# Gated attention plus mixture of experts: one expert's rows sorted by products instead of two, and both its layers run first

## What is computed

```python
x = x + tanh(g_xattn) * smoothquant_expert(layernorm(x), gate_up, down)   # int8-like, per batch element
s = layernorm(x)                                   # 1024 rows of 256
gates = softmax(s @ w_gate)                        # 8 experts
e = argmax(gates); slot = number of earlier tokens with the same e; kept while slot < 128
h = gelu(dispatched[e] @ w1[e])                    # 128 x 256 @ 256 x 1024
y = h @ w2[e]                                      # 128 x 1024 @ 1024 x 256
x = x + tanh(g_ffn) * gates[e] * y                 # for the kept tokens
```

## Time and profile before

| | us |
|---|---|
| three runs, median (lowest, highest) | 118.71 (117.54, 119.16) |
| the profiled execution | 118.51 |
| its span | 116.7 |
| PE busy in the span | 101.5 (87%) |
| DVE busy | 86.3 (74%) |
| ACT busy | 76.2 (65%) |
| POOL busy | 53.9 (46%) |
| PE's share of the chain that ended last | 38% |

### The profile page before, as it was taken

One profiled execution on the slowest core, in us unless ns is written; L12 is line 12 of the kernel. 1 busy time (PEld: TensorE's weight loads), 2 busy tenths in 40 slices (PEclk: granted clock), 3 DMA queues, 4 the chain that ended last, 5 costly groups with the idle time before them and its releaser, 6 DMA issues.

```text
span 116.7 us, 2279 instructions
## 1 busy us (share of the span) xinstructions
PE 101.5 (87%) x770; PEld 88.0 (75%) x770; DVE 86.3 (74%) x229; ACT 76.2 (65%) x158; POOL 53.9 (46%) x117
## 2 busy tenths in 40 slices
PE   0979679999889889987999969999999999999930
PEld 0459358988557657886999759899999989999820
DVE  5637989899987899981049759969688696939540
ACT  0464789999896989894737739585573739376000
POOL 7858765669968878867730000621030303011041
PEclk9999999999999999999999999999999999999999
DMA  3999998999984903379226999899999900101011
GB/s 73 345 308 323 150 198 314 338 367 373 364 293 89 341 25 139 134 205 336 101 83 205 287 351 323 308 350 280 346 297 361 325 0 0 51 0 45 0 45 45
DMA packets 16074, 24.86 MB, mean 213 GB/s; under 512 B 1352, under 2 KB 13641, under 8 KB 15040
## 3 DMA queue, kind: packets, MB, share of 16 engines
q1 hardware_dynamic: 14208, 21.60, 59.5%
q0 software_dynamic: 768, 2.08, 4.9%
q10 hardware_dynamic: 1088, 1.05, 2.8%
HBM read 20.50 MB, written 4.28 MB: 212 GB/s over the span
## 4 chain that ended last, share of the span: by engine, by line
PE 38%; POOL 14%; DMA 13%; DVE 12%; ACT 11%; issue 7%; SPq 2%; POOLq 1%; DVEq 0%
PE bk L1133 19%; PE bk L1145 10%; POOL slot_rows L406 6%; DMA x<-in_x 6%; DMA gr<-slot_rows 5%; PE bk L1147 5%; DVE am L706 3%; ACT wide_a L519 3%; POOL row L392 2%; DMA slot_rows<-row,slot 2%; ACT wide_b L528 2%; POOL sc L350 2%; PE bk L1159 2%; PE bk L998 1%; DVE am L762 1%
## 5 line engine op out<-in xcount | busy, mean ns | idle before, releaser
L471 POOL DMA_INDIRECT out<-scrow,gr x8 | 8.6, 1075 | 45.9 <-DVE scrow L926 44.5
L1133 PE MATMUL bk<-rows_w,w_sb 128*128 128x128 f32 x192 | 22.8, 275 | 0.9 <-DVE rows_w L916 0.9
L1133 PEld LDWEIGHTS bk<-rows_w,w_sb 128*128 128x128 f32 x192 | 22.1, 192 | 1.3 <-DVE rows_w L916 1.2
L1145 PE MATMUL bk<-w2p,hh 128*128 128x512 f32 x56 | 20.5, 406 | 0.2 <-DVE hl L843 0.2
L831 DVE TENSOR_TENSOR w2p<-w_sb,w2p 128x1024 fp32r<-128x1024 f32 x12 | 14.0, 1218 | 7.9 <-POOL begun L461 6.8
L1147 PE MATMUL bk<-w2p,hl 128*128 128x256 f32 x56 | 15.7, 280 | 0.0
L584 ACT ACTIVATE w2p<-w_sb 128x1024 fp32r<-128x1024 f32 x12 | 12.0, 1048 | 5.4 <-PE bk L1147 5.4
L652 ACT ACTIVATE hh<-bk 128x512 fp32r<-128x512 f32 x16 | 9.5, 592 | 7.1 <-PE bk L1133 7.1
L1145 PEld LDWEIGHTS bk<-w2p,hh 128*128 128x128 f32 x56 | 10.5, 188 | 2.5 <-issue 0.3
L976 PE MATMUL bk<-identb,upper 128*128 128x512 bf16 x26 | 8.2, 437 | 3.0 <-POOL upper L297 3.0
L1147 PEld LDWEIGHTS bk<-w2p,hl 128*128 128x128 f32 x56 | 10.6, 189 | 0.0
(11 more groups left out here) (163 smaller groups left out, 232.2 us busy)
## 6 DMA issues: line engine op xcount, KB each, us to landing
w_sb<-in_w SPq DMA_DIRECT2D x12, 1024.0 KB, 6.4
slot_rows<-empty SPq DMA_DIRECT2D x1, 1068.0 KB, 13.9
cw<-in_ctx_gu ACTq DMA_DIRECT2D x4, 256.0 KB, 5.5
x<-in_x SPq DMA_DIRECT2D x4, 256.0 KB, 4.6
cw<-in_w SPq DMA_DIRECT2D x1, 1024.0 KB, 5.8
out<-row SPq DMA_DIRECT2D x4, 256.0 KB, 2.6
x<-in_w SPq DMA_DIRECT2D x1, 1024.0 KB, 6.1
wide_a<-in_w SPq DMA_DIRECT2D x1, 1024.0 KB, 8.2
```

The source lines that it names most:

```text
L1133: ins = nc.tensor.matmul(HB[e % 2][:, m, n * C:(n + 1) * C], wv[:, k, o:o + P], xgT[:, e % B, k], start=(k == 0), stop=(k == K - 1))
L1145: nc.tensor.matmul(YB[e % 2], hh[:, e % 2, n], w2p[:, e % 2, n].rearrange("p a d -> p (a d)"), start=(n == 0), stop=False)
```

## The change

`NEAR` goes from 2 to 1. Expert 1 is no longer sorted by products but comes by the gather, like experts 2 to 7, with a transfer and a semaphore (`second_here`) of its own, ahead of the others. The one-hots are 128 x 256 and each `dispatch(b)` has 8 products instead of 16. The order at the joint is rewritten on PE and on DVE.

```diff
-    NEAR = 2
+    NEAR = 1
...
-        hot = wide_b[:, :, 2 * T:4 * T].rearrange("p b (j s) -> p b j s", j=J)
+        hot = wide_b[:, :, 2 * T:2 * T + J * NEAR * C].rearrange("p b (j s) -> p b j s", j=J)
...
+            sp.dma_start(gr[:, 1:2], sc_rows[:, 1:2]).then_inc(second_here, 16)
             sp.dma_start(gr[:, 2:4], sc_rows[:, 2:4]).then_inc(rows_here, 16)
-            sp.dma_start(gr[:, 0:2], sc_rows[:, 0:2]).then_inc(rest_here, 16)
+            sp.dma_start(gr[:, 0:1], sc_rows[:, 0:1]).then_inc(rest_here, 16)
             sp.dma_start(gr[:, 4:E], sc_rows[:, 4:E]).then_inc(rest_here, 16)
...
+                if e == 1:
+                    pool.wait_ge(second_here, 16)
...
             split_low(0)
-            split_low(1)
...
-                dve.wait_ge(rows_here, 16)
+                dve.wait_ge(second_here if e == 1 else rows_here, 16)
...
+            hidden_low(0)
+            expert_in(1)
+            expert_turned(1)
             expert_in(2)
-            hidden_low(0)
+            expert_turned(2)
+            split_low(1)
             expert_in(3)
+            hidden_low(1)
+            dve.wait_ge(second_here, 16)
             dve.wait_ge(rows_here, 16)
             dve.wait_ge(rest_here, 32)
...
-            expert_turned(2)
-            hidden_low(1)
             dve.wait_ge(exp_ready, 1)
...
             hidden(0, 0)
             hidden(0, 1)
-            hidden(1, 0)
-            hidden(1, 1)
-            slots_turn(2)
             expert_out(0, 0)
             expert_out(0, 1)
+            slots_turn(1)
+            hidden(1, 0)
+            slots_turn(2)
+            hidden(1, 1)
             for e in range(1, E - 1):
```

More of the change, by code:

```diff
@@ L185, in gated_smoothquant_moe_kernel @@
         rows_scattered = sem("rows_scattered")
-        rows_here = sem("rows_here")
+        rows_here, second_here = sem("rows_here"), sem("second_here")
         rest_here = sem("rest_here")
```

## The result

The changed kernel takes 119.81 us (median of 20 runs, 118.96 to 121.76), the kernel before 118.66 (20 runs, 117.54 to 119.37). The ratio is 1.0104, 95% interval 1.0073 to 1.0135: 1.2 us slower, less than the 2% that the text ahead called telling, but clear of no change. The profiled execution took 119.19 us, its span is 117.4.

What follows compares the result with a forecast made beforehand. PE, busy throughout from 69.43 to 111.00 us, was taken as the bound, so only its entry counts. The walk's +1.07 less POOL's 0.25 gives +0.8 on 118.51: 119.3 us, range 118.2 to 121.0.

Steps and rivals of the forecast that it cites:

- the meeting point: Start of expert 3's first layer on PE, behind which the order is unchanged; forecast to move from 76.32 to 77.39.
- Step 1: PE's sorting products ahead of expert 0, halved: its first layer starts at 57.2 instead of 57.44, the rest hidden behind ACT.
- Step 2: Expert 0's second layer ahead of expert 1's first: PE idles 1.89 us for DVE, starts at 62.93, ends at 65.95.
- Step 3: Expert 1 gathered, turned and copied: PE's added turn (0.23) and round trip put its first layer at 66.69.
- Rival C: Expert 1's gather lands late, at 67.3, so PE's turn waits: +1.9 us, 121.2 us; chance 0.03.
- Step 4: PE's walk from expert 1's first layer to expert 3's: reaches it at 77.39 instead of 76.32, +1.07 us.
- The two covers on DVE: hidden_low(1) and the copy of expert 3's rows are ready before PE wants them, by about 1 us each.
- Step 5: Halved one-hots on DVE beside POOL's scatters: shorter overlap at the first scatter relieves POOL's chain, -0.25 us.
- rival B: POOL's relief is larger, -0.7 us across its scatters: 118.9 us, read as no change; chance 0.13.
- Rival A: Thinned products and the new standstill drop PE's clock to 1.2 GHz: about +2.5 us, 121.8 us; chance 0.12.
- the two halves "3.2 us later": Within Rival A: at the lower clock expert 0's two first-layer halves end 3.2 us later, at 64.2.

Runs made afterwards that it cites:

- experiment 1: Changed kernel with 14 idle products on PE in the gaps between the sorting products; ratio 1.0092 to the kernel before, 120.40 us.
- experiment 2: Kernel before with only the new PE and DVE order, both experts still sorted by products; ratio 1.0021, 118.80 us.
- experiment 5: Kernel of experiment 1 with seven more idle products on PE in the standstill ahead of expert 0's second layer; ratio 1.0064, 119.24 us.
- experiment 3: Changed kernel with one-hots of full width again (128x512, only expert 0's half used); ratio 1.0151 to the kernel before, 120.40 us.
- experiment 4: Kernel before without expert 1's sorting products, order as before, expert 1 working on other rows; ratio 0.9995, 118.58 us.
- experiment 6: Kernel before with DVE's copy of expert 2's rows and hidden_low(1) ahead of the softmax; ratio 0.9912, 117.40 us.
- experiment 7: Kernel of experiment 6 with expert 0's low part also ahead of expert 1's weight split on DVE, PE's order untouched; ratio 0.9828, 116.31 us.
- experiments 8: Kernel of experiment 7 with the first one-hot moved on DVE from ahead of expert_out(2) to behind place(1); ratio 0.9886, 117.15 us.
- experiment 9: Kernel of experiment 1 without DVE's wait for POOL's last scatter ahead of the weight split; ratio 1.0076, 119.11 us.

## Why the prediction held, and where it was off

The forecast was 119.3 us, within 2%; the median is 119.8, inside the range. Its sign was right, its size of +0.8 us should have been +1.2. In the two profiled executions the meeting point moved by 1.05 us: the forecast's 0.82, plus 0.36 for the second layer that the clock cut in two, less 0.21 for a larger relief of POOL, and 0.08 left over. Two misses of opposite sign brought the sum closer than its terms.

- **Step 1**, start of expert 0: forecast 57.2, and 0.7 earlier with POOL's relief and the earlier start of that execution. Measured 57.12. That this is the 57.2 of the forecast is luck; by its own terms it should have been 56.5. The step failed through the clock: the last sorting group took 2.04 us, so ACT waited for PE (0.71 us ahead of 56.68) and not PE for ACT. With the clock held (experiment 1) the first layer starts at 56.58.
- **Step 2**, the second layer waits for DVE: right. It starts 3.17 us after DVE's release, forecast 3.10. The standstill was forecast at 1.89 us; it is 0.28, because PE's slow halves filled it. With fills between the sorting products it is 1.94 and without the sorting change 1.77.
- **Step 3**, the added turn and round trip: 66.26 - 65.51 = 0.75, forecast 0.74. Expert 1's gather landed after 2.1 us, in time. Rival C is out.
- **Step 4**, the walk to the meeting point: 10.54 us from 66.26 to 76.80, forecast 77.39 - 66.69 = 10.70 in the view that counts a start 0.16 later, so 10.54. The two covers on DVE held: PE has no idle from 66.26 to the meeting point. Experiments 2 and 5 put the price of expert 1's gather at 1.01 us and that of the order at 0.11, together 1.12 for the forecast's 1.07.
- **Step 5**, POOL's relief: forecast 0.25, measured 0.46: 0.22 at the first scatter (1.26 instead of 1.48), which was forecast near 1.1, and 0.18 at the small operation beside the last one-hot (0.24 instead of 0.42), of which the forecast says nothing. The first is the shorter one-hot's (experiment 3). The second is not: it goes with one-hots of full width too, once PE has fewer sorting products (experiment 4), because the last one-hot then starts earlier and no longer meets the operation. In experiment 5, where fills hold PE up, the last one-hot meets it again and it takes 0.38. So the relief is larger, as in rival B, at two thirds of its size, but rival B looked for all of it at the scatters.
- **Rival A**, the clock, given 0.12, came true. The mean clocks of the twenty runs are 0.944 to 0.985; of the 69 runs of the kernel before that stand beside the experiments, 56 have 0.988 or more. Of the two causes that it named, the thinned products are enough (experiment 4); the fall came before the new standstill. Its price was not as written: forecast +2.5 us over the rest, in the profiled execution +0.36. The fall began earlier than assumed, at 52 us, and was over at 59, so that most of it lay in a stretch where PE would have waited for DVE anyway. The failed step is the chance, and with it the two halves "3.2 us later": they took 4.73 us instead of 3.84 and ended at 61.85, 0.8 later than the forecast's 61.04, or 1.7 later than in experiment 1 when both are counted from the first scatter (18.13 us against 16.42).

So the loss is three terms: +1.07 us for the new walk (the turn, its round trip and the standstill), -0.46 from POOL, and the clock, +0.36 where it falls early and 1.4 where it falls over the second layer (experiment 1). With the clock held the ratio is 1.006 instead of 1.010, with intervals that overlap.

The forecast also passed over the largest thing in its own rows. PE's 0.88 us wait and DVE's 1.98 us wait for the last gather were read as a place that the change rewrites, and not as slack that a two-line reordering frees; experiment 6 took 0.9% out of it and experiment 7 1.7%.

What stays open: why 8 runs of the changed kernel took 120.2 us and more. The clock may have fallen late in them, as in experiment 1, or for longer, as in 3, or near the start as well, as in the profiled execution of 8; or it is what lengthens runs of experiment 9 at full clock. Their mean clocks, 0.947 to 0.980, do not tell these apart, and no profile shows one of them. Open are also the three long runs of experiment 2 and how the 0.5% of experiment 3 divides.

## What to carry to other kernels

Before products are taken off an engine that is waiting, ask what keeps its clock up: thinned work ahead of the dense part can let the clock fall, and what that costs depends on where it lands. A wait makes everything ahead of it cheap, so see first what the last wait ahead of the dense stretch depends on; here it was a copy queued behind an unrelated wait for a transfer, and putting the copy and the low part first gained 1.7% where the whole change lost 1.0%. Two-input VectorE work beside a chain of small GpSimd operations had a price wherever it was put (experiments 8 and 9): look at which small operation it will lie over before moving it. And compare executions from a common instruction onward, since they can lie 0.4 to 1 us apart before the first changed one.

## What the runs showed that was not expected

- The clock fell some 0.8 us after PE had taken up dense work again, behind a standstill of 1.94 us (experiment 1), and in experiment 2 it stayed at 1.00 over the same kind of standstill of 1.77 us. What went ahead of the two differs: sorting products with fills there, full sorting products here. Three runs of experiment 2 with mean clocks near 0.975 may have had the fall too.
- A fall of the clock cost nothing (experiment 4), 0.4 us (the changed kernel) or 1.4 us (experiment 1), by what lay under it.
- POOL's operations on 128 x 2 elements grew two- to more than threefold when they started under a DVE subtraction or comparison of two SBUF operands: 0.24 to 0.71 us, 0.72 to 1.55, 0.19 to 0.68. The scatter beside one grew from 1.26 to 1.48 only. The Trainium skill (GPSIMD Engine Reference, Key points) names that contention for two-input DVE instructions; the trace agrees, and adds that small operations suffer most, since each is held until the DVE instruction ends.
